# A decoder block on one core: write strength from one narrow product, experts in alternation, smaller VectorE steps, new order tables

## The chip, the cores and the metric

The kernel runs on one core of a Trainium2 chip. A core has TensorE (PE, matrix products into PSUM), VectorE (DVE), ScalarE (ACT), GpSimd (POOL) and SyncE (SP, which issues DMAs here); they run side by side and wait for each other through semaphores. The metric is the device time of one execution in microseconds. Three executions of the kernel before took 1631.0 to 1631.2 us, median 1631.13.

## The reference, cut to what matters

The input x has 4 batches of 1024 tokens with 256 channels. Three sublayers follow one another, each added to x after a layer norm: a gated delta rule with 16 heads of 16 channels, a differential cross attention over 64 context tokens, and a convolution with a mixture of 8 experts and a feed-forward part. The change touches the gates of the first and the sum of the third:

```python
p = hidden @ cond_in_W                      # then a rotating scan over time, and an rms norm: cond
deltas = cond @ delta_W                     # 3 x 256 columns for q, k, v and 16 for beta
bd = bd * jax.nn.sigmoid(beta_ramp_logit)
ctrl = hidden @ ctrl_W + ctrl_b             # q, k, v, decay (16), beta (16), gate (256)
beta = jax.nn.sigmoid(bet_l + bd)           # write strength, one per head and token
g = jax.nn.sigmoid(dec_l)                   # decay, one per head and token
def step(Sst, inp):
    qt, kt, vt, bt, gt = inp
    Sd = gt[..., None, None] * Sst
    kS = jnp.einsum('bhk,bhkv->bhv', kt, Sd)
    Snew = Sd + jnp.einsum('bhk,bhv->bhkv', kt, bt[..., None] * (vt - kS))
    ot = jnp.einsum('bhk,bhkv->bhv', qt, Snew)
    return (Snew, ot)
...
rw = jnp.sum(jax.nn.one_hot(top_i, E, dtype=x1.dtype) * top_w[..., None], axis=-2)
ye = jax.nn.silu(jnp.einsum('bsd,eod->bseo', x1, expert_w) + expert_b)
combined = jnp.einsum('bse,bseo->bso', rw, ye)
```

## The kernel before

The 1024 tokens are cut into 8 blocks of 128 tokens of all 4 batches, 512 columns in the layout with channels on partitions. `turns` walks i from -1 to 8. In turn i three pieces of work are interleaved: the front part of block i+1 (marked + in the table `ORDER`: layer norm, the rotating scan, the projections, the causal convolution), the recurrent part of block i (no mark), and attention and experts of block i-1 (marked -). In turns 1 to 6 all three run. I call turn i "block i"; it ends with `x1_`, VectorE's sum of the residual with the output product of block i (line 1201).

What sets the order of the work is written out by hand: `ORDER` has one list of steps for each engine, and an engine runs its steps in exactly this order, waiting at each for the events that it needs (`up`) and telling its own (`fin`). The table `KEEP` has the program issue dummy products (`keep`, line 1440, a 128x128 product of the identity with itself) ahead of certain steps of TensorE.

The front part has PSUM bank 7 for itself. Each of its products waits until the one before has been read out, so on TensorE they stand far apart and other work lies between. They are `turn1` (transposes), `rot`, `unrot`, `gate`, `cond`, `db` and `proj.0` to `proj.7`. `proj.0` and `proj.1` give the logits of the write strength, each of the 16 columns repeated 16 times, so that `beta` comes out in the layout of k and v (256 rows for 16 heads). `proj.2` to `proj.7` are q, k and v. ScalarE takes exp of the two, VectorE (`beta_`, line 1024) adds one over 128x1024, and ScalarE takes ln and exp of that (`blog`, lines 611 and 612): sigmoid(x) is exp(-ln(1 + exp(-x))). `db` computes the decay logits with tokens on partitions: for each batch two products of `hT` with `ctrl`, one of the condition with `dw`, and one that adds the bias, each of 32 columns. VectorE bounds them (`edb`, line 1051), ScalarE takes exp, and in the next turn, as their first steps, VectorE adds one (`spread`, line 1069), ScalarE takes ln into `lgc` (line 645), and GpSimd expands this into `xpand` and `lrep`, which TensorE's `decay` and `grow` read.

In the recurrent part, `sum.0` to `sum.3` are the products for the norms of q and k (they read squares that ScalarE makes, line 631), `raw.0` to `raw.7` are products of keys with keys and queries, `am` scales them, and `solve.0` to `solve.15` invert a triangular matrix by small VectorE steps. After `solve.15` each of 8 chunks of 16 tokens goes through `z`, `zc`, `d1`, `m`, `cs`, `s`, `co`, `o`: `z`, `d1`, `cs` and `co` are TensorE's, the others VectorE's, and `s` of a chunk gives the state that `d1` of the next reads.

In the third part, `sc`, `max`, `pt`, `pv` and `av` are attention (scores, softmax, transposes, values, VectorE's difference of two attentions), and `moe.0` to `moe.31` the expert products, two for each pair u of experts, u from 0 to 15. ScalarE takes silu of a pair's result into one of four buffers, and VectorE's `acc` adds the pair's two experts to `comb`, the sum of their batch, one instruction each:

```python
b, ep = u // 4, u % 4
up("moe_act", u + 1)
for e2 in range(2):
    ins = stt(comb[:, b, :], src, wgt, comb[:, b, :], ALU.mult, ALU.add)
```

All instructions of four pairs in a row add to the same `comb[:, b, :]`, and each waits for the one before. `o_` and `av` are also chains of four dependent VectorE instructions, each run as one step.

## Time and profile before

| | us |
|---|---|
| median of three executions | 1631.13 |
| the profiled execution | 1631.66 |
| its span, first to last instruction | 1629.9 |
| TensorE busy | 1526.6 |
| VectorE busy | 1220.2 |
| ScalarE busy | 845.6 |
| GpSimd busy | 204.8 |

The span is the time from the first to the last instruction on the core; the execution's own time is 1.8 us longer. Busy time is the time in which an engine ran an instruction. A product of 32-bit numbers appears as two records, so a count of 52 dummy records is 26 products at most; two records of one product overlap, and a distance between starts tells what a product costs in a full stream. Some records of the bias products, in 16-bit numbers, are missing.

### The profile page before, as it was taken

What the parts mean: (1) busy time and instruction counts of PE and PEld (TensorE: products, weight loads), DVE (VectorE), ACT (ScalarE), POOL (GpSimd) and SP (SyncE); (2) the same over time, 40 slices, a digit from 0 to 9 for tenths busy, and PEclk for the clock granted to TensorE, in tenths of its full rate; (3) what the DMA queues carried; (4) which work ended last, traced back from release to release, by engine and by line L of the source; (5) the groups of instructions that cost most, each with busy time, mean ns of one, the idle gap of its engine ahead of it and who ended that gap; (6) DMA issues with size and microseconds to landing.
All of it is one profiled execution on the core that took longest, in us unless ns stands there. A gap on an engine that the chain in (4) does not pass through costs nothing.

```text
span 1629.9 us, 39565 instructions
## 1 busy us (share of the span) xinstructions
PE 1526.6 (94%) x16532; PEld 1040.2 (64%) x16598; DVE 1220.2 (75%) x3201; ACT 845.6 (52%) x1612; POOL 204.8 (13%) x212
## 2 busy tenths in 40 slices
PE   5899899999999999999999999999999999999888
PEld 3475677656766577656765577656766577757665
DVE  6256868886788878886798877877798867875553
ACT  1354454655646474655646474655646474534333
POOL 0030212011300112011300112011200112010000
PEclk7999989999999999999999999999999999999999
DMA  5010001000100001000100001000100001000000
GB/s 228 1 27 27 3 1 28 27 2 14 28 6 23 2 14 27 28 2 15 27 13 16 2 15 27 27 2 4 38 1 15 2 14 28 15 2 14 1 1 13
DMA packets 20217, 31.75 MB, mean 19 GB/s; under 512 B 1480, under 2 KB 17864, under 8 KB 19784
## 3 DMA queue, kind: packets, MB, share of 16 engines
q1 hardware_dynamic: 20040, 29.22, 6.2%
q8 instruction: 132, 2.16, 0.6%
q14 instruction: 45, 0.37, 0.1%
HBM read 20.81 MB, written 8.39 MB: 18 GB/s over the span
## 4 chain that ended last, share of the span: by engine, by line
PE 77%; DVE 17%; ACT 3%; issue 3%; DVEq 0%
PE bank L1781 15%; PE bank L1518 7%; PE bank L1729 6%; PE bank L1397 6%; PE four L1590 4%; PE bank L1440 4%; PE bank L1719 4%; PE bank L1520 3%; PE bank L1422 3%; PE bank L1705 3%; PE four L1642 2%; PE four L1609 2%; PE four L1658 2%; PE bank L1429 2%; PE four L1422 2%
## 5 line engine op out<-in xcount | busy, mean ns | idle before, releaser
L1781 PE MATMUL bank<-w_sb,cs 128*128 128x512 f32 x512 | 257.8, 614 | 0.1
L791 ACT ACTIVATE cs<-bank 128x512 f32<-128x512 f32 x128 | 76.2, 595 | 203.5 <-remote 130.3
L510 POOL TENSOR_TENSOR decayed<-state,pk 128x512 f32<-128x512 f32 x64 | 69.7, 1090 | 716.4 <-DVE state L1165 716.4
L1440 PE MATMUL bank<-c_sb 128*128 128x128 f32 x1070 | 141.1, 286 | 5.3 <-DMA c_sb<-in_consts 5.3
L1440 PEld LDWEIGHTS bank<-c_sb 128*128 128x128 f32 x1070 | 134.4, 200 | 17.7 <-issue 10.9
L1729 PE MATMUL bank<-vx_sb,cs 128*128 128x136 f32 x1024 | 136.7, 286 | 8.1 <-ACT cs L745 8.1
L745 ACT COPY cs<-bank 128x512 f32<-128x512 f32 x128 | 74.9, 585 | 127.0 <-PE bank L1719 127.0
L1345 DVE SCALAR_TENSOR_TENSOR cs<-cs,rwt 128x256 f32<-128x256 f32 x224 | 117.9, 526 | 26.9 <-ACT cs L791 14.8
L1729 PEld LDWEIGHTS bank<-vx_sb,cs 128*128 128x128 f32 x1024 | 125.7, 192 | 17.0 <-ACT cs L745 11.6
L1781 PEld LDWEIGHTS bank<-w_sb,cs 128*128 128x128 f32 x512 | 89.5, 189 | 73.0 <-issue 64.1
L1518 PE MATMUL bank<-hT,w_sb 128*128 128x512 f32 x256 | 124.4, 608 | 9.1 <-ACT pre L595 6.2
L1719 PE MATMUL bank<-c_sb,cs 128*128 128x128 f32 x512 | 81.2, 281 | 22.4 <-ACT cs L745 14.7
L738 ACT ACTIVATE cs<-cs 128x1024 f32<-128x1024 f32 x64 | 67.4, 1052 | 63.8 <-DVE cs L1243 63.8
L1238 DVE TENSOR_REDUCE pkc<-bank 128x8 f32<-128x512 f32 x128 | 82.7, 682 | 21.1 <-PE bank L1705 20.9
L1037 DVE SCALAR_TENSOR_TENSOR qkv<-pre,l_sb,qkv 128x512 f32<-128x512 f32 x144 | 97.5, 746 | 0.0
L1243 DVE TENSOR_TENSOR cs<-bank,pkc 128x512 f32<-128x512 f32 x128 | 81.9, 681 | 20.7 <-PE bank L1719 20.7
L1165 DVE SCALAR_TENSOR_TENSOR state<-four,c_sb,decayed 128x128 f32<-128x128 f32 x256 | 71.9, 344 | 31.7 <-PE four L1642 29.4
L1719 PEld LDWEIGHTS bank<-c_sb,cs 128*128 128x128 f32 x512 | 55.6, 141 | 59.6 <-issue 48.7
L545 ACT ACT_TABLE_LOAD x66 | 84.7, 1283 | 1.2
L1705 PE MATMUL bank<-kbx,cs 32*128 32x256 f32 x512 | 83.6, 400 | 0.2 <-ACT cs L733 0.2
L1397 PE MATMUL bank<-cs,w_sb 128*128 128x256 f32 (+1 forms) x320 | 80.1, 389 | 0.4 <-DVE cs L1290 0.4
L1148 DVE SCALAR_TENSOR_TENSOR shared<-four,c_sb 128x256 f32<-128x256 f32 x128 | 55.5, 475 | 32.8 <-PE four L1609 32.5
(243 smaller groups left out, 2990.5 us busy)
## 6 DMA issues: line engine op xcount, KB each, us to landing
xt<-in_x SPq DMA_DIRECT2D x8, 512.0 KB, 4.8
vscr<-qkv SPq DMA_DIRECT2D x8, 512.0 KB, 2.6
vT<-vscr SPq DMA_DIRECT2D x32, 128.0 KB, 4.4
Tm<-in_x SPq DMA_DIRECT2D x8, 512.0 KB, 3.8
out<-cs SPq DMA_DIRECT2D x8, 512.0 KB, 2.9
w_sb<-in_weights SPq DMA_DIRECT2D x1, 3656.0 KB, 19.1
w_sb<-in_weights SPq DMA_DIRECT2D x1, 1840.0 KB, 9.1
cs<-in_scratch SPq DMA_DIRECT2D x3, 256.0 KB, 9.5
```

Source lines behind the costliest of these rows:

```text
L545: nc.scalar.preload_act_table_set(name)
L1037: ins = stt(dst, pre[:, n % 4, :, t:TB + t], L("conv", 4 * n + t, 4 * n + t + 1), dst, ALU.mult, ALU.add)
L1238: step.append(link(red(mx[:, a, :], sc[a], AX.X, ALU.max)))
L1243: fin("psub", tt(prob[:, 4 * a:4 * a + 4, :, :].rearrange("p h f n -> p f h n"), sc[a].rearrange("p (f h) n -> p f h n", f=2), mx[:, a, :] ...
L1345: ins = stt(comb[:, b, :], src, wgt, comb[:, b, :], ALU.mult, ALU.add)
L1397: last = mm(dst, lhs(k), rhs(k), start=k == 0, stop=k == n - 1)
L1440: mm(bank[7 if i > 0 else 6][:, 0:P], ident, ident, start=True, stop=True)
L1518: last = mm(dst, ctrl[:, k, cc:cc + P], hT[:, k, :], start=k == 0, stop=False)
L1705: last = mm(bank[4 + a][:, 256 * f:256 * f + 256], qx[r:r + 32, f, b * TB:b * TB + TB], kbx[r:r + 32, f, b, :], start=True, stop=True)
L1719: last = nc.tensor.transpose(bank[6][:, h * P:h * P + P], prob[:, 4 * n + h, :, :].rearrange("p f n -> p (f n)"), ident)
L1729: last = mm(bank[6][:, 34 * h:34 * h + 136], probT[:, h, :], vx_sb[:, at:at + 136], start=True, stop=True)
L1781: mm(dst, x1T[:, k, b * TB:b * TB + TB], ew[:, k, ep * 512:ep * 512 + 512], start=k == 0, stop=False)
```

## The change

**Write strength.** `proj` has six steps instead of eight, for q, k and v alone. `db` now computes decay and write strength together as one product with channels on partitions: 32 rows (16 decay, 16 beta) by 512 columns. ScalarE takes exp with the bias in it, VectorE bounds and adds one, ScalarE takes ln; the result `lgT` lies in 32 rows of `rota`. Two new kinds of TensorE steps read it: `btr` transposes it to tokens on partitions for the decay (VectorE copies that into `lgc`), and `brep.0` and `brep.1` multiply it by a constant selector matrix that repeats each of the 16 rows 16 times, after which one exp on ScalarE gives `beta`. All this is in the front part; the steps `spread` of VectorE and ScalarE at the start of the turn, and `beta_`, are gone.

```diff
                 def db():
                     up("cond")
-                    if i == 0:
-                        pe.wait_ge(ld_b3, 48)
-                    for b in range(B):
-                        dst = bank[7][:, b * 32:b * 32 + 32]
-                        for k in range(KC):
-                            mm(dst, hT[:, k, b * TB:b * TB + TB], ctrl[:, k, 1280:1312], start=k == 0, stop=False)
-                        mm(dst, rotb[:, b * TB:b * TB + TB], dw[:, 1024:1056], start=False, stop=False)
-                        last = bias(dst, "db")
-                    fin("db_ps", last)
+                    emptied()
+                    fin("db_ps", controls(bank[7][0:32, :], 1024, 32))
...
+                def btr():
+                    up("lg")
+                    emptied()
+                    for b in range(B):
+                        last = nc.tensor.transpose(bank[7][:, 32 * b:32 * b + 32], lgT[:, b * TB:b * TB + TB], ident[0:32, 0:32])
+                    fin("lt_ps", last)
...
+                def brep(g):
+
+                    up("lg")
+                    emptied()
+                    fin("brep_ps", mm(bank[7][:, :], C("sel")[0:32, P * g:P * g + P], lgT, start=True, stop=True))
```

`controls` is the three products that `proj` also uses. `emptied` waits for whatever step last used bank 7; before, each step named that step itself, so their order was fixed in the code.

**Experts.** A pair u is now of batch 2 * (u // 8) + u % 2, so that neighbouring pairs add to different batches, and a step `acc.u.e2` is one instruction.

```diff
+        def expert(u):
+
+            return 2 * (u // 8) + u % 2, u % 8 // 2
...
+                        if e2:
+                            ch.wait(added[u % 2])
                         else:
-                            if not e2:
-                                up("moe_acc", u)
-                            ins = stt(comb[:, b, :], src, wgt, comb[:, b, :], ALU.mult, ALU.add)
+                            up("moe_acc", u - 1)
+                        ins = stt(comb[:, b, :], src, wgt, comb[:, b, :], ALU.mult, ALU.add)
```

**Smaller steps.** `o_` and `av` are likewise cut into four steps of one instruction each, which the order places singly.

**Order.** `ORDER` and `KEEP` are new throughout; a full turn has 20 dummy products instead of 25, turns -1, 0, 7 and 8 have 103, 140, 51 and 114 instead of 84, 117, 74 and 110. Two lines of TensorE's list:

```diff
-        sum.0 sum.1 decay sum.2 +turn1.0 -turn2.0 +turn1.1 grow -turn2.1 -qx.0 sum.3 -sc.0.0 -qx.1 -sc.0.1 vturn raw.0
...
+        sum.0 sum.1 decay -turn2.0 sum.2 grow -turn2.1 -qx.0 sum.3 -sc.0.0 -qx.1 -sc.0.1 vturn raw.0 raw.1 -sc.1.0
```

TensorE at the seam between two full turns, before. The first row is the output product, 1440 the dummies, 1543 `sum`, 1560 and 1561 `decay`, 1469 `turn1`, 1429 `turn2`, 1568 `grow`:

```order
L1422 MATMUL four<-w_sb,kn 128x256 x8
L1440 MATMUL bank<-c_sb 128x128 x8
L1543 MATMUL four<-rota,c_sb 128x512
L1543 MATMUL four<-rotb,c_sb 128x512
L1560 MATMUL four<-Tm,c_sb 128x512
L1561 MATMUL four<-Tm,c_sb 128x512
L1543 MATMUL four<-rota,c_sb 128x512
L1469 MATMUL bank<-c_sb,xt 128x128 x4
L1429 MATMUL bank<-c_sb,cs 128x128 x4
L1469 MATMUL bank<-c_sb,xt 128x128 x4
L1568 MATMUL four<-c_sb,mk 128x128 x8
```

And now (1441 the output product, 1568 `sum`, 1585 and 1586 `decay`, 1448 `turn2`, 1459 the dummies, 1593 `grow`):

```order
L1441 MATMUL four<-w_sb,kn 128x256 x8
L1568 MATMUL four<-rota,c_sb 128x512
L1568 MATMUL four<-rotb,c_sb 128x512
L1585 MATMUL four<-Tm,c_sb 128x512
L1586 MATMUL four<-Tm,c_sb 128x512
L1448 MATMUL bank<-c_sb,cs 128x128 x4
L1568 MATMUL four<-rota,c_sb 128x512
L1459 MATMUL bank<-c_sb 128x128 x3
L1593 MATMUL four<-c_sb,mk 128x128 x8
```

The dummies ahead of `sum.0` are gone, three stand ahead of `grow`, and `turn1` has moved to a later place.

TensorE around the first step `z.0` of the recurrence in a full turn, before (1518 and 1520 `proj.1`, 1719 `pt.15`, 1415 and 1422 attention's output product, 1609 `z`, 1729 `pv.7`):

```order
L1518 MATMUL bank<-hT,w_sb 128x512 x2
L1520 MATMUL bank<-rotb,w_sb 128x512
L1719 MATMUL bank<-c_sb,cs 128x128 x4
L1415 MATMUL bank<-bias,ones 128x512
L1422 MATMUL bank<-w_sb,cs 128x256 x4
L1609 MATMUL four<-kn,M 32x128 x16
L1729 MATMUL bank<-vx_sb,cs 128x136 x8
```

And now (1514 `cond`, 1746 `pt.11`, 1634 `z.0` and `z.1`, 1756 `pv.5`, 1732 `sc.7`, 1667 `cs.0.0`, 1530 and 1531 the new `db`):

```order
L1514 MATMUL bank<-qkv,c_sb 128x512
L1746 MATMUL bank<-c_sb,cs 128x128 x4
L1634 MATMUL four<-kn,M 32x128 x16
L1756 MATMUL bank<-vx_sb,cs 128x136 x8
L1732 MATMUL bank<-kbx,cs 128x256 x4
L1634 MATMUL four<-spare,M 32x128 x16
L1667 MATMUL four<-rq,shared 64x4x16 x8
L1530 MATMUL bank<-hT,w_sb 32x512 x2
L1531 MATMUL bank<-rotb,w_sb 32x512
```

`z.0` has moved ahead of `db`, all `proj` and the last three steps `pv`.

VectorE in the last scaling step `am.3` and after it, before (1102 to 1104 `am`, 1251 to 1256 `av.2`, 994 and 1000 the scan of the front part, 1116 and 1120 `solve.0`, 1238 and 1243 `max`):

```order
L1104 TENSOR_TENSOR mk<-four,pk 128x2x8x16
L1251 RECIPROCAL pkc<-bank 128x16
L1253 TENSOR_SCALAR pkc<-pkc,small 128x8
L1254 TENSOR_TENSOR cs<-bank,pkc 128x256
L1256 TENSOR_TENSOR cs<-cs 128x128
L994 TENSOR_TENSOR rotb<-bank,sinT 128x512
L1000 SCALAR_TENSOR_TENSOR qkv<-rota,zc,rotb 128x128 x4
L1116 STREAM_TRANSPOSE Tm<-M 128x16x32 x2
L1120 MEMSET Tm 128x4x16
L1238 TENSOR_REDUCE pkc<-bank 128x8 x2
```

And now (987 `turn1`, 1118 and 1122 `solve.0`, 1261 to 1271 the four steps of `av.1`, 1135 and 1139 steps of the solve):

```order
L1106 TENSOR_TENSOR mk<-four,pk 128x2x8x16
L987 COPY hT<-bank 128x512
L1118 STREAM_TRANSPOSE Tm<-M 128x16x32 x2
L1122 MEMSET Tm 128x4x16
L1261 RECIPROCAL pkc<-bank 128x16
L1135 TENSOR_TENSOR M<-Tm 128x56
L1267 TENSOR_SCALAR pkc<-pkc,small 128x8
L1139 TENSOR_TENSOR Tm<-Tm,M 128x4x14
L1269 TENSOR_TENSOR cs<-bank,pkc 128x256
L1135 TENSOR_TENSOR M<-Tm 128x104
L1271 TENSOR_TENSOR cs<-cs 128x128
```

The solve starts two attention steps earlier and its steps alternate with those of `av`.

## Rows read from the trace of the kernel before

**Rows 1.** The page: busy time of the engines, and the chain by engine.

```profile
PE 1526.6 (94%) x16532; PEld 1040.2 (64%) x16598; DVE 1220.2 (75%) x3201; ACT 845.6 (52%) x1612; POOL 204.8 (13%) x212
...
PE 77%; DVE 17%; ACT 3%; issue 3%; DVEq 0%
```

**Rows 2.** Stretch, us, busy PE, PEld, DVE, ACT, POOL (instructions), PE clock, DMA share, GB/s.

```profile
405.90:590.60 184.70, 178.84 (x1982) 119.53 (x1991) 148.63 (x390) 104.24 (x200) 25.53 (x26) 0.99 0.06 16
590.60:773.50 182.90, 177.04 (x1981) 117.71 (x1989) 148.64 (x389) 104.23 (x200) 25.54 (x26) 1.00 0.06 16
```

**Rows 3.** The same of line 1440 alone (dummies), block 3: PE and PEld.

```profile
590.60:773.50 182.90, 6.27 (x52) 5.91 (x51) 1.00 0.06 16
```

**Rows 4.** TensorE's timeline in block 3: start, us, instruction, idle before.

```profile
658.66 0.53 PE L1530 MATMUL bank<-w_sb,hT 128*128 128x32 f32 x4
...
661.37 2.10 PE L1729 MATMUL bank<-vx_sb,cs 128*128 128x136 f32 x16
663.31 1.88 PE L1518 MATMUL bank<-hT,w_sb 128*128 128x512 f32 x4
...
665.88 0.60 PE L1429 MATMUL bank<-c_sb,cs 128*128 128x128 f32 x4
```

**Rows 5.** Timelines at the seam to block 3: TensorE, VectorE, ScalarE, GpSimd.

```profile
590.37 1.95 PE L1440 MATMUL bank<-c_sb 128*128 128x128 f32 x16
592.82 1.12 PE L1543 MATMUL four<-rota,c_sb 128*128 128x512 f32 x2 [0.51 <-ACT rota L631]
...
594.64 1.02 PE L1560 MATMUL four<-Tm,c_sb 128*128 128x512 f32 x2
...
590.57 1.29 DVE L1201 TENSOR_TENSOR xr<-four,Tm 128x512 f32<-128x512 f32 x2 [2.69 <-PE four L1422]
...
591.99 0.26 ACT L645 ACTIVATE lgc<-edb 128x64 f32<-128x64 f32 x1 [5.00 <-DVE edb L1069]
...
592.32 1.22 POOL L470 TENSOR_TENSOR Tm<-lgc,c_sb 128x256 f32<-128x256 f32 x2 [13.04 <-ACT lgc L645]
```

**Rows 6.** The solve's end, `pt.11` and `z.0` in block 3; the page's softmax row.

```profile
667.74 1.93 DVE L1124 STREAM_TRANSPOSE M<-Tm 128x512 f32<-128x512 f32 x2
...
651.88 0.63 PE L1719 MATMUL bank<-c_sb,cs 128*128 128x128 f32 x4 [0.20 <-ACT cs L745]
...
671.98 0.69 PE L1609 MATMUL four<-kn,M 64*32 64x128 f32 x32
...
L1238 DVE TENSOR_REDUCE pkc<-bank 128x8 f32<-128x512 f32 x128 | 82.7, 682 | 21.1 <-PE bank L1705 20.9
```

**Rows 7.** Busy time in three stretches of block 3, columns as in rows 2.

```profile
607.00:635.00 28.00, 28.00 (x380) 22.15 (x381) 19.73 (x44) 15.29 (x35) 10.86 (x13) 1.00 0.19 40
635.00:665.00 30.00, 27.12 (x208) 19.93 (x205) 28.39 (x68) 14.36 (x24) 0.00 (x0) 1.00 0.00 1
...
680.00:695.00 15.00, 15.00 (x205) 9.39 (x204) 13.27 (x36) 10.18 (x18) 1.06 (x1) 1.00 0.01 2
```

**Rows 8.** VectorE's timeline: dependent sums (1345, 1175) and independent ones (1165).

```profile
721.50 3.81 DVE L1345 SCALAR_TENSOR_TENSOR cs<-cs,rwt 128x256 f32<-128x256 f32 x7
...
726.39 1.12 DVE L1175 SCALAR_TENSOR_TENSOR M<-four,c_sb,M 128x128 f32<-128x128 f32 x3
727.59 1.13 DVE L1165 SCALAR_TENSOR_TENSOR state<-four,c_sb,decayed 128x128 f32<-128x128 f32 x4
```

**Rows 9.** TensorE's timeline in block -1: `db`, `proj.0`, `proj.1`.

```profile
46.00 0.63 PE L1530 MATMUL bank<-w_sb,hT 128*128 128x32 f32 x4
...
49.35 1.92 PE L1518 MATMUL bank<-hT,w_sb 128*128 128x512 f32 x4
...
52.91 1.99 PE L1518 MATMUL bank<-hT,w_sb 128*128 128x512 f32 x4 [0.78 <-ACT hid L589]
```

**Rows 10.** ScalarE's timeline around a switch of table.

```profile
691.28 1.28 ACT L545 ACT_TABLE_LOAD   x1
692.58 0.84 ACT L775 ACTIVATE cs<-bank,l_sb 128x256 f32<-128x256 f32 x2
```

362 lines of the change are left out of this document (185 added, 177 removed), and 3 rows, old and new, of the table KEEP.

## The prediction

> **What bounds the kernel now.** The page first: TensorE is busy for 94% of the span, VectorE for 75%, ScalarE for 52%, and in the chain that ended last TensorE has 77% and VectorE 17% [rows 1]. A busy TensorE need not be doing useful work here, because the program also issues dummy products. So I next cut the span at the residual sum `x1_`, which ends a block of 128 tokens. Blocks 1 to 6, where all pipeline halves run, last 182.9 to 184.7 us (three have the clock of the first of rows 2 and 184.4 to 184.7 us, three that of the second and 182.9 to 183.0). Block 3 holds 177.0 us of TensorE in 182.9 us, so 5.9 us are idle [rows 2], and 6.3 us of its busy time are dummies [rows 3]. These 12.2 us I call the slack of a block. VectorE is idle for 34 us of it, so on average TensorE is the bound. It is not so everywhere: from 607 to 635 us TensorE never stops and VectorE has 19.7 of 28 us; from 635 to 665 us VectorE has 28.4 of 30 us and TensorE idles for 2.9 [rows 7].
>
> **The work that goes.** Durations below are distances between starts in a full stream, not busy times. A `proj` (three products of 512 columns) runs from 663.31 to 665.88: 2.57 us, so 2.6. The old `db`, with its 16 small products, runs from 658.66 to 661.37: 2.71 us [rows 4]. Removed per block: two `proj` and the old `db`, 2 x 2.6 + 2.7 = 7.9 us. Added: a `db` of the same three 512-column products with only 32 output rows. The trace shows no product of this form; above stands `proj` with 2.6, below the old `db` less its four bias products, about 2; I take 2.6, since the columns that stream are the same. Two selector products contract over 32 rows; the nearest rows are `sum.0` and `sum.1` (512 columns each), which start at 592.82 and are done when `decay` starts at 594.64, so 1.8 for two [rows 5]. Four transposes of 32 columns are not in the trace either: above, four of 128 columns take 0.60 us [rows 4], below, nothing; I take 0.5, as each loads weights like those. Sum 4.9, **saved 3.0 us per block** (2.9 to 4.1 with the ends). It counts where TensorE is the bound, in blocks 1 to 6: 18 us.
>
> ScalarE loses two passes over 128x1024 and gains a few over 32x512, VectorE trades one pass over 128x1024 and two over 128x64 for one over 32x512 and one copy. Both engines have idle time for that; I cost it at nothing, and count what it does at the seam below. Where ScalarE's cover is gone, as in block -1, it is worth under 1 us.
>
> **The seam between blocks.** After the output product ends (about 590.4) TensorE runs eight dummies and then idles 0.51 us before `sum.0` at 592.82. What ended this wait is ScalarE's square at 592.15, and ahead of that in ScalarE's queue stands the logarithm of the decay at 591.99, which waits for VectorE's `edb`, behind `x1_` [rows 5]. The change takes this logarithm to the block before, so the square no longer waits for `x1_`, and `sum.0` and `sum.1` can follow the output product at once. Next late is `decay`: it needs GpSimd's expansion, which now starts after `x1_` itself (591.86) rather than at 592.32 and takes 1.2 us, so about 593.1 to 593.2 instead of 594.64. TensorE waits there for 1 us or so. The seam gives back 1.4 us; `turn1`, which filled part of it, goes to a later place, so in slack I credit 0.6 us.
>
> **VectorE's stretch.** `z.0` needs the end of the triangular solve (two transposes, 667.74 to 669.67) and started at 671.98 [rows 6]. In the new order the solve starts before the fourth softmax step and its steps lie between those of the attention sums, so that VectorE's waits from 607 to 635 us (8.3 us by rows 7) fill with it. Two softmax steps (four passes of the kind of line 1238 each, 82.7 / 128 = 0.65 us a pass, 2.6 us), two attention sums (four dependent small instructions, 1.2 to 1.6 us by rows 8) and two small steps, some 8 us together, come behind the solve. The solve then ends 16 us or so earlier in the block, near 653, and TensorE gets to the new place of `z.0` at about the same time (its old neighbour `pt.11` stood at 651.88). Splitting helps too: three dependent sums of 128x128 take 1.12 us, four independent ones 1.13, so 0.39 against 0.26 us from start to start, while expert sums stand at 3.81 / 7 = 0.54 us each [rows 8]. If the same 0.13 us goes from each, alternation between two batches saves up to 32 x 0.13 = 4 us of VectorE per block, the interleaving of the attention sums with the solve perhaps 2. VectorE is idle elsewhere, so this reaches the time only through the 2.9 us that TensorE idles from 635 to 665 us and the short waits before expert products. I take 1.2 us.
>
> **Dummies.** 20 instead of 25 per block, each 0.24 us of TensorE (52 records, 6.27 us, two records each): 1.2 us, if the waits that they covered are gone.
>
> Slack thus falls by 0.6 + 1.2 + 1.2 = 3.0 of 12.2 us (bounds -1 and 8), and a full block by 6.0: **6 x 6.0 = 36 us**.
>
> **The ends.** In block -1 everything goes through bank 7 in turn, product and read-out. The old `db` holds it from 46.00 to 49.35, each of the two write-strength products 3.56 us (49.35 to 52.91, 0.78 of it the read-out) [rows 9]: 10.5 us. New: `db` 2.6 + 0.8, the transposes with VectorE's copy 0.9, two selector products with read-out 2 x 1.7: 7.7. Gain 2.8, less 0.3 for the logarithm over 32x512 where one over 128x64 stood: 2.5 us. Block 0 is set by the recurrence; half of the 3.0 us, less half of what 23 more dummies cost, is nothing (range 4 either way). Block 7 has no next block, so no work is removed; 23 dummies less are worth between 0 and 5.5 us, I take 2. Block 8: nothing, 2 either way.
>
> Sum: 36 + 2.5 + 2 = 40.5. The profiled execution took 1631.66 us, 1.8 above its span and 0.5 above the median of 1631.13. 1631.66 - 40.5 = 1591.2, or 1590.6 on the median's footing: **1591 us**.
>
> **A rule that speaks against it.** The new ScalarE order switches to the table of silu, back for the logarithm and to silu again shortly before `pw.0`, two more switches there and two fewer at the tail. A switch takes 1.28 us and the next operation starts 1.30 us after it (691.28 to 692.58) [rows 10]. ScalarE has 4.8 of 15 us free there, from 680 to 695 us [rows 7], so 2.6 us are hidden. The Trainium skill's page "ScalarE: Activation LUTs" (section "What ACT_TABLE_LOAD costs") states 1283 ns plus a drain of about 1380 ns, 2.66 us for each switch. The first part agrees with the row, the drain is not to be seen in it. By the row the sum stands at 1591; by the page, the two switches would be 5.3 us, and if the 2.7 us more lay on the path of all six blocks, 1607.
>
> **Rivals.**
> (a) *More slack goes.* If the solve fills VectorE's waits fully and the expert sums stop holding ScalarE, slack falls by 6 instead of 3: 6 x 3 = 18 us more, 1573. For it: TensorE's needs are met by VectorE alone from 635 to 665 us. Against: some of the 5.9 us idle are short gaps after missing records of the bias products, which no order removes.
> (b) *Only the work goes.* Slack stays at 12.2 us, because `z.0` and its recurrence now stand in the stretch where VectorE had 28.4 of 30 us, and what the seam gains is waited for at `decay` and `grow`. Gain 18 + 2.5 = 20.5, thus 1611.
> (c) *The queue turns against it; slower.* `z.0` now stands ahead of `pv.5` and of the scores behind it in TensorE's queue. If VectorE's 8.3 us of waits are not filled, the solve ends 8 us after TensorE arrives. Each block then loses 8.3 us at that place against 3.0 saved and 1.2 of dummies: 6 x 4.1 = 25 us more, 1656. It decides from a wait of 4.2 us at `z.0` on. Against it: `raw.7`, on which the solve's input rests, also stands some six steps earlier.
> (d) *Nothing happens*: a loop through VectorE sets each block and the saved products become waits or dummies; 1631. Against: from 607 to 635 and from 680 to 695 us TensorE is busy without a gap [rows 7].
> (e) *The clock*: fewer useful products and no dummies where the order guesses wrong let TensorE's granted clock fall to its lower level once in each block, as in three of the six now, which are 1.5 us or more longer [rows 2]. Three more blocks cost 4.5 us: inside the range of the forecast, so no case of its own.
>
> **How the numbers follow.** Forecast 0.52; (a) 0.20; (b) 0.19; (c) 0.05; (d) 0.04. The forecast's own terms move by 6 x 0.5 for the work, 6 x 2 for slack about it and 4 for the ends, so 1580 to 1605; the range takes in most of (b) and half of (a): **1576 to 1611**. A measurement of this kernel can tell 0.2%, about 3 us, from no change. Faster: the forecast, (a), (b): 0.91. Same: (d): 0.04. Slower: (c): 0.05.
>
> **What would show it.** In the changed profile: full blocks of 176 to 179 us between `x1_` and `x1_`; `sum.0` right behind the output product and 1 us or so of idle before `decay`; the transposes that end the solve some 60 to 62 us after `x1_` instead of 77, and less than 1 us of idle before `z.0`; dummies 20 per block; expert sums near 0.4 us each. I am wrong if TensorE's idle time per block exceeds 8 us (then look before `z.0`, `decay`, `grow` and in the tail behind the last expert product, where three chunks of the recurrence now stand instead of two), or if `db` takes much more or less than 2.6 us.

## The result and the profile after

The changed kernel takes **1622.11 us** (median of 5 runs, 1616.38 to 1627.61) against 1631.13 (5 runs beside it, 1630.29 to 1634.54): ratio 0.9941, interval 0.9913 to 0.9968. It is faster by 9 us, not by the 40 that were forecast, and outside the range. A second set of 6 runs, made beside the later experiments, gave 1617.57 us (0.9921, interval 0.9900 to 0.9942). The profiled execution is the slowest of the first set, 1627.61 us, with a span of 1625.8.

The page of the changed kernel, the lines that answer to [rows 1]:

```profile
PE 1519.0 (93%) x16376; PEld 1024.8 (63%) x16376; DVE 1179.9 (73%) x3193; ACT 830.7 (51%) x1594; POOL 209.2 (13%) x212
...
PE 72%; DVE 22%; ACT 3%; issue 3%; POOL 0%; DVEq 0%; ACTq 0%
```

VectorE did less (1180 for 1220 us), yet its share of the chain grew from 17% to 22%. The blocks 1 to 7 of the changed kernel, from `x1_` to `x1_`, columns as in [rows 2]:

```profile
219.15:403.74 184.59, 176.93 (x1953) 116.19 (x1952) 143.35 (x388) 102.63 (x198) 26.37 (x26) 0.98 0.06 16
403.74:588.52 184.78, 177.15 (x1953) 116.23 (x1952) 143.40 (x388) 102.55 (x198) 26.34 (x26) 0.98 0.06 16
588.52:769.85 181.33, 173.71 (x1953) 114.53 (x1952) 143.19 (x388) 102.56 (x198) 26.36 (x26) 1.00 0.06 16
769.85:953.02 183.17, 175.58 (x1953) 115.36 (x1952) 143.26 (x388) 102.66 (x198) 26.36 (x26) 0.99 0.06 16
953.02:1137.63 184.61, 176.95 (x1953) 116.22 (x1952) 143.34 (x389) 102.66 (x198) 26.36 (x26) 0.98 0.06 16
1137.63:1322.37 184.74, 177.06 (x1953) 116.13 (x1952) 143.34 (x388) 102.54 (x198) 26.37 (x26) 0.98 0.05 13
1322.37:1488.34 165.97, 155.38 (x1938) 111.74 (x1937) 121.41 (x331) 81.35 (x163) 23.03 (x25) 0.98 0.06 14
```

Two things are to be seen. Only block 3 had TensorE's full clock, and it lasts 181.3 us, where the like block before lasted 182.9 (second of [rows 2]): **1.6 us less, not 6.0**. And the others are longer by 1.7 us for each fall of the granted clock to 1.2 GHz. One fall lasts 3.4 us here, so it takes 0.01 from the mean clock of a block: two falls at 0.98, one at 0.99, nine in blocks 1 to 6, where before there were three. In the profiled run those six extra falls ate all that the six blocks had gained: they last 1103.2 us together, before 1102.4.

What is left of the gain stands outside the six blocks. The stretch up to `x1_` of block 0, in the kernel before, the changed kernel and its second profile (`after_again`, below), columns as in [rows 2]:

```profile
0.00:222.96 222.96, 182.19 (x1974) 125.43 (x1975) 133.71 (x357) 85.34 (x154) 25.84 (x29) 0.92 0.15 52
0.00:219.15 219.15, 185.31 (x2005) 127.92 (x2006) 131.60 (x357) 83.73 (x153) 25.46 (x29) 0.93 0.15 52
0.00:212.41 212.41, 177.79 (x2005) 123.39 (x2006) 131.45 (x357) 83.58 (x153) 25.43 (x29) 0.97 0.15 53
```

TensorE was at the lower clock for 34.1, 30.7 and 13.7 us of it. If each such microsecond costs half a microsecond, the most it can, the three stretches would last 206, 204 and 206 us at the full clock (an estimate from these rows). So the 4 to 11 us gained there are mostly clock, and a gain of the change itself is not shown there.

The new steps on TensorE in block 3, `db`, `btr` and `brep.0` (start, us, instruction):

```profile
657.36 1.90 PE L1530 MATMUL bank<-hT,w_sb 128*32 128x512 f32 x4
...
668.30 0.43 PE L1550 MATMUL bank<-c_sb,rota 32*128 32x32 f32 x4
...
669.64 1.12 PE L1558 MATMUL bank<-rota,c_sb 32*128 32x512 f32 x2
```

`db` runs until `pt.12` at 660.06: 2.7 us. The next steps start 0.36 us behind `btr` and 1.05 behind each `brep`. Added: 2.7 + 0.4 + 2.1 = 5.2 for a forecast of 4.9; saved 7.9 - 5.2 = **2.7 us of work, against 3.0**. This term held.

The seam at 588.52, the answer to [rows 5]:

```profile
588.32 1.02 PE L1568 MATMUL four<-rota,c_sb 128*128 128x512 f32 x2
...
591.24 1.13 PE L1585 MATMUL four<-Tm,c_sb 128*128 128x512 f32 x2 [1.03 <-POOL Tm L481]
...
596.34 2.02 PE L1593 MATMUL four<-c_sb,mk 128*128 128x128 f32 x16 [1.16 <-DVE pk L1084]
```

`sum.0` stands right behind the output product, `decay` waits 1.03 us for GpSimd, as forecast, and starts 2.7 us behind `x1_` (4.1 before). But `grow` waits another 1.16 us for VectorE.

From `x1_` to `pt.4`, to `pt.11` and to the block's end, first the kernel before, then the changed one (both block 3, full clock):

```profile
590.57:626.97 36.40, 35.42 (x388) 27.02 (x386) 29.18 (x72) 24.73 (x55) 10.59 (x13) 1.00 0.15 30
626.97:651.88 24.91, 23.23 (x188) 15.44 (x185) 22.53 (x53) 9.90 (x16) 2.47 (x3) 1.00 0.00 1
651.88:773.53 121.65, 118.44 (x1409) 75.31 (x1419) 96.96 (x266) 69.59 (x129) 12.47 (x10) 1.00 0.05 15
```

```profile
588.52:627.72 39.20, 36.72 (x414) 27.77 (x413) 34.88 (x83) 23.48 (x52) 13.12 (x16) 1.00 0.13 28
627.72:651.77 24.05, 20.87 (x148) 13.72 (x149) 23.53 (x62) 13.09 (x24) 0.00 (x0) 1.00 0.00 1
651.77:769.85 118.08, 116.12 (x1392) 73.05 (x1392) 84.78 (x245) 65.99 (x122) 13.24 (x10) 1.00 0.05 15
```

TensorE idles 2.5 us up to `pt.4` (1.0 before), 3.2 to `pt.11` (1.7 before) and 2.0 behind it (3.2 before; 1.3 us of that are nine gaps of 0.15 us where records are missing, see `before_less_work`). With 4.95 us of dummies (line 1459, 40 records) for 6.27 [rows 3], the slack of a block is 12.6 us, where it was 12.2. It was to fall by 3.0.

### The profile page after: what moved, and what is told of

The parts are those of the page before. It is cut to its first block, busy times and chain, and to the rows that moved or that the text cites. A ratio compares the mean times of both kernels' runs of the same rounds, so it can differ in the third digit from the quotient of the medians.

```text
span 1625.8 us, 39269 instructions
## 1 busy us (share of the span) xinstructions
PE 1519.0 (93%) x16376; PEld 1024.8 (63%) x16376; DVE 1179.9 (73%) x3193; ACT 830.7 (51%) x1594; POOL 209.2 (13%) x212
## 4 chain that ended last, share of the span: by engine, by line
PE 72%; DVE 22%; ACT 3%; issue 3%; POOL 0%; DVEq 0%; ACTq 0%
PE bank L1808 14%; PE bank L1756 6%; PE bank L1530 5%; PE bank L1416 5%; PE bank L1746 4%; PE bank L1459 4%; PE bank L1732 4%; PE four L1615 4%; PE bank L1441 3%; PE bank L1531 2%; PE four L1634 2%; PE bank L1523 2%; PE four L1683 2%; DVE qkv L1038 2%; PE bank L1422 2%
## 5 line engine op out<-in xcount | busy, mean ns | idle before, releaser
L1808 PE MATMUL bank<-w_sb,cs 128*128 128x512 f32 x512 | 246.9, 602 | 0.0
L521 POOL TENSOR_TENSOR decayed<-state,pk 128x512 f32<-128x512 f32 x64 | 74.4, 1163 | 925.5 <-DVE state L1167 925.5
L1808 PEld LDWEIGHTS bank<-w_sb,cs 128*128 128x128 f32 x512 | 95.1, 191 | 90.9 <-issue 80.1
L1364 DVE SCALAR_TENSOR_TENSOR cs<-cs,rwt 128x256 f32<-128x256 f32 x224 | 98.7, 482 | 70.2 <-ACT cs L797 70.1
L1530 PE MATMUL bank<-hT,w_sb 128*128 128x512 f32 (+1 forms) x224 | 109.7, 613 | 6.2 <-ACT pre L598 4.0
L1732 PE MATMUL bank<-kbx,cs 32*128 32x256 f32 x512 | 87.4, 400 | 0.7 <-ACT cs L739 0.7
```

Of the source, the lines that this page charges most:

```text
L1530: mm(dst, ctrl[:, k, at:at + n], hT[:, k, :], start=k == 0, stop=False)
L1732: last = mm(bank[4 + a][:, 256 * f:256 * f + 256], qx[r:r + 32, f, b * TB:b * TB + TB], kbx[r:r + 32, f, b, :], start=True, stop=True)
L1808: mm(dst, x1T[:, k, b * TB:b * TB + TB], ew[:, k, ep * 512:ep * 512 + 512], start=k == 0, stop=False)
```

## The experiments

Sixteen more runs were made, one of them of the changed kernel again. Each kernel is compared with the kernel before on the same chip; the medians of that one were 1631.1 to 1633.6 us.

**1. The clock.** The theory to test: falls of the granted clock, brought on by many short waits of TensorE, ate the gain. `after_again` is the changed kernel as it is.

> The changed kernel unchanged, beside the others on this chip. If the falls of the clock come by where a block happens to stand when the chip looks, then this profile shows the same three places (47, 119 and 170 us behind x1_) in other blocks than the first profile did, and the runs spread over 6 us or more again, in the order of their mean granted clock, 1.4 to 1.5 us for each 0.001 of it. If they are this kernel's own, each in its block, the falls stand in the same blocks as before.

1617.57 us (1615.54 to 1623.44). The falls stood 47, 119 and 170 us behind `x1_` again, but in blocks 2, 4 and 5, five of them, where the first profile had them in 1, 2, 4, 5 and 6. The eleven runs of both sets follow their mean clock closely, though not in strict order, from 0.979 with 1627.61 to 0.987 with 1615.54 to 1616.38: some 1.4 us per 0.001, and one fall is 0.001. So the place of a fall belongs to the kernel, and whether it happens is another matter in each block and run.

`after_dummies_in_waits`:

```diff
+KEEP = {(1, -1, "pt", 5): 1, (1, -1, "pv", 2): 2, (1, -1, "pt", 6): 2, (1, -1, "pt", 7): 3,
+        (1, -1, "pt", 9): 2, (1, 0, "d1", 6): 2, (1, 0, "co", 7, 0): 1,
...
```

> The changed kernel with 13 dummies more in each of blocks 1 to 6, put where TensorE waits anyway: ahead of pt.5 (1), pv.2 (2), pt.6 (2), pt.7 (3), pt.9 (2), d1.6 (2) and co.7.0 (1). In the changed kernel's profile the granted clock falls to 1.2 GHz nine times in these blocks, seven of them 47 and 170 us behind x1_. The clock theory says that these falls ate the gain: the seven go, each is worth 1.7 us (a block with none lasts 181.3, with one 183.1, with two 184.7), so 12 us less than the profiled run of the changed kernel and 6 to 8 less than its median: 1614 to 1616. The rival, new waits ate it: falls or not, blocks do not get shorter than 181.3 us, and the median moves by under 3 us, because in the median run of the changed kernel the clock is about that of the kernel before.

1609.86 us (1607.28 to 1613.29), ratio 0.9874 (0.9855 to 0.9893). Five blocks last 181.4 to 181.5 us, one 183.1 with one fall. In the changed kernel's block 1, the 6.8 us ahead of the fall and the fall itself; then the same place with the dummies (columns as in [rows 2]):

```profile
259.60:266.40 6.80, 4.74 (x35) 3.78 (x36) 6.52 (x17) 2.23 (x3) 0.00 (x0) 1.00 0.00 0
266.40:269.80 3.40, 3.40 (x8) 1.63 (x6) 2.43 (x5) 1.82 (x3) 0.00 (x0) 0.51 0.02 5
```

```profile
252.20:259.00 6.80, 6.48 (x51) 5.57 (x51) 6.52 (x17) 2.23 (x4) 0.00 (x0) 1.00 0.01 2
259.00:262.50 3.50, 3.50 (x22) 2.54 (x21) 3.46 (x8) 1.89 (x3) 0.00 (x0) 1.00 0.00 0
```

TensorE was busy for 4.74 of 6.8 us, in pieces between waits, and its clock fell; with 6.48 us it did not. The median is 8 to 12 us under the changed kernel's two. The profiled runs differ from its two by 8.3 and 20.3 us; the six blocks hold 5.9 and 13.0 us of that, and the stretch up to block 0, where these dummies do not stand, 0.6 and 7.4. Blocks got no shorter than 181.4, so the clock explains nothing of the 26 us by which six full blocks miss the forecast (6 x 6.0 less 6 x 1.6).

`after_no_dummies` drops the three entries of `KEEP` for blocks 1 to 6.

> The changed kernel without its 20 dummies in blocks 1 to 6 (4.5 us of TensorE per block). If they only stand in waits, a block with a full clock stays at 181.3 us and idle time takes their place (7.8 to 12.3 us idle per block), and what changes is the clock: falls at the seam behind x1_ come on top, one or two in each block, 6 x 1.7 to 12 x 1.7 us, so 1632 to 1642. The rival, dummies cost what they last: 6 x 4.5 = 27 us less, 1595.

1628.79 us (1625.87 to 1637.86, 12 runs). Idle time took the place of the dummies (11.7 us per block for 7.6 and 5.0), and there were 13 falls in the six blocks, four of them of 6.8 us. In block 1, where the first fall stands 176 us behind `x1_`, the last expert product starts 154.6 us behind `x1_` in both kernels and the output product 177.5 us (177.7 with the dummies): the dummies cost at most 0.2 us of a block, and they buy 7 to 11 us of clock. My third slack term, "5 fewer dummies 1.2 us", was thus worth nothing: what a dummy covers is a wait.

**2. The new VectorE steps.** `after_steps_together`, in VectorE's order:

```diff
-... solve.0 -av.1.0 solve.1.0 -av.1.1 solve.1.1 ... o.1.0 -av.7.0 o.1.1 -av.7.1 o.1.2 ... -acc.0.0 -acc.1.0 -acc.0.1 -acc.1.1
+... solve.0 -av.1.0 -av.1.1 -av.1.2 -av.1.3 solve.1.0 ... o.1.0 o.1.1 o.1.2 o.1.3 -av.7.0 ... -acc.0.0 -acc.0.1 -acc.1.0 -acc.1.1
```

> The changed kernel with the four steps of each attention sum, the four of each chunk's output and the two of each expert sum put together again on VectorE, at the place of the first. It undoes the interleaving alone. If finer steps are worth what I gave them (0.13 us for each dependent step, 32 expert sums and the attention sums: 4 to 6 us of VectorE per block, 1.2 us of the time), a full block lasts 182.5 us and VectorE is busy 5 us more of it: about 7 us more than the changed kernel, 1629. If VectorE's slack takes it, under 2 us.

1638.53 us (12 runs), ratio 1.0026 (1.0006 to 1.0047): 0.3% slower than the kernel before. Its stretches from `pt.4` to `pt.11` and the whole block 3:

```profile
620.70:647.04 26.34, 21.05 (x149) 13.88 (x149) 25.33 (x64) 13.10 (x24) 0.00 (x0) 1.00 0.00 1
...
581.55:765.98 184.43, 174.00 (x1950) 114.69 (x1952) 147.61 (x389) 102.79 (x198) 25.57 (x26) 1.00 0.06 16
```

A block at full clock lasts 184.4 us: interleaving is worth **3.1 us**, of which 2.3 between `pt.4` and `pt.11`, where VectorE works 1.8 us longer and TensorE waits 2.1 us more. I had given it 1.2 in all. (The order was made for single steps; what an order made for whole steps would take was not tried, so 3.1 us is what interleaving is worth in this order.)

`after_no_alternation`:

```diff
-            return 2 * (u // 8) + u % 2, u % 8 // 2
+            return u // 4, u % 4
...
-                            up("moe_acc", u - 1)
+                            up("moe_acc", u)
```

> The changed kernel with experts in the old order, all of one batch before the next, and each expert's two sums one behind the other, as they then must be. If the alternation is what keeps ScalarE's read-out of the experts, and so TensorE, from waiting, TensorE idles again behind router.0, 0.5 us or more in each block, and the median is 3 to 6 us over the changed kernel's. My sum held VectorE idle enough there: nothing, within 2 us at the same clock.

1623.34 us at clocks of 0.982 to 0.988. Blocks 1, 3 and 5 last 183.9 us with one fall, where the changed kernel's blocks with one fall last 182.9 to 183.2: 0.7 to 1.0 us per block for the alternation. On VectorE the expert sums of the changed kernel stand closer:

```profile
720.50 2.45 DVE L1364 SCALAR_TENSOR_TENSOR cs<-cs,rwt 128x256 f32<-128x256 f32 x6
722.87 0.34 DVE L1181 SCALAR_TENSOR_TENSOR M<-four,c_sb,M 128x128 f32<-128x128 f32 x1
```

That is 2.45 / 6 = 0.41 us each, where seven dependent ones took 0.54 [rows 8]. Over the whole run the median distance from start to start of neighbouring sums is 0.40 us, 0.52 before and 0.52 again in `after_no_alternation`. So the 0.13 us for each sum came as forecast. (One sum still lasts 0.48 us; neighbours that do not wait for each other overlap.) It takes 2 us off VectorE in a block, and 0.7 to 1.0 us of that reach the time.

**3. Where TensorE's work counts.** `before_less_work` leaves out two of the three products of each write-strength projection of the kernel before:

```diff
+                    if j < 2:
+                        fin("proj_ps", mm(dst, ctrl[:, 0, cc:cc + P], hT[:, 0, :], start=True, stop=True))
+                        emptied[0] = ("pre_sb", i, j + 1)
+                        return
```

> The kernel before, in its own order, with each of its two 128-wide write-strength products cut from five passes of matmul to one of 512 columns: about 2 x 2.1 = 4.3 us of TensorE per block less, nothing added or moved; the write strength it computes is not that of the reference. If TensorE's work reaches the time one for one, as my sum had it: 6 x 4.3 = 26 us and some 4 more in block -1, 1601 to 1605. If VectorE's and ScalarE's chains around them set the pace, most of it turns into waits: 1620 or more.

1616.89 us (1610.97 to 1624.23), ratio 0.9910 (0.9886 to 0.9934). Its block 3, full clock:

```profile
582.72:763.52 180.80, 175.21 (x1982) 116.23 (x1981) 148.52 (x389) 104.28 (x200) 25.54 (x26) 1.00 0.06 16
```

180.8 for 183.0 us. My expectation had the cut too large: a projection has three products, and between starts it now takes 0.85 and 0.93 us (655.51 to 656.36, 657.63 to 658.56) for 2.57 and 2.67, so 3.4 us are gone and not 4.3. **2.2 of the 3.4 us arrive**; most of the rest stands as two new waits behind the cut, 0.20 us ahead of a softmax transpose and 0.84 ahead of `z.0`. This kernel also shows the dense expert products and their neighbours with almost no gap, where the trace of before has nine gaps of 0.15 us each, 1.3 us, with nothing changed there: records are missing. So the true slack before was about 11 us rather than 12.2, and it rose by more than the 0.4 us above.

`after_less_late`, `after_less_tensor`, `after_less_vector` and `after_less_both` cut work in the changed kernel:

```diff
-                    for k in range(KC):
+                    for k in range(1 if at < 768 else KC):
                         mm(dst, ctrl[:, k, at:at + n], hT[:, k, :], start=k == 0, stop=False)
```

```diff
-                    fin("rot_ps", over_k(bank[7][:, :], lambda k: cin[:, k, n * P:n * P + P], lambda k: hT[:, k, :]))
+                    fin("rot_ps", mm(bank[7][:, :], cin[:, n, n * P:n * P + P], hT[:, n, :], start=True, stop=True))
...
-                        step.append(link(red(mx[:, a, :], sc[a], AX.X, ALU.max)))
+                        step.append(link(red(mx[:, a, :], sc[a][:, :, 0:NK // 4], AX.X, ALU.max)))
```

(the gate likewise with one product; the first cut is `after_less_late`, the second `after_less_tensor`, the third `after_less_vector`.)

> The changed kernel with the six projections of one product less each (the second half of the contraction left out, so q, k and v are not the reference's): 6 x 0.86 = 5.2 us of TensorE less in each block, between 662 and 701 us of block 3, where TensorE has 39.2 of 40 us and VectorE 33.5. That is where the removed products stood. If TensorE is the bound there, blocks of 176.1 us. If the work behind it waits for VectorE again, a part goes into waits: half, as in the kernel before with two shorter products (2.2 of 4.3 us), would be 178.7 us.

1609.36 us, 0.9856 (0.9831 to 0.9881). From `pt.11` to `turn3.1` and on to `moe.8`, the changed kernel, then this one. By the order, four of the shortened projections (`proj.0` to `proj.3`) lie in the first stretch and two in the second:

```profile
651.77:689.98 38.21, 38.01 (x597) 24.16 (x596) 29.86 (x81) 23.35 (x47) 3.18 (x3) 1.00 0.10 30
689.98:716.01 26.03, 25.43 (x266) 15.63 (x261) 22.19 (x71) 15.02 (x25) 1.16 (x1) 1.00 0.01 1
```

```profile
635.69:671.25 35.56, 34.79 (x588) 22.59 (x587) 29.71 (x81) 22.84 (x47) 3.18 (x3) 1.00 0.11 32
671.25:699.02 27.77, 25.52 (x257) 15.38 (x257) 22.25 (x71) 15.02 (x25) 1.16 (x1) 0.94 0.00 1
```

In the first, 2.6 of 4 x 0.86 = 3.4 us arrive; TensorE idles 0.8 us for 0.2, since `z.5` now waits 0.58 us for VectorE. In the second, of 1.7 us nothing does: without its fall of 1.7 us it would last 26.1 us, as before the cut, with 2.3 us idle for 0.6. The longest of its new waits is `d1.4`'s, for VectorE's state:

```profile
682.22 0.46 PE L1651 MATMUL four<-state,kq 64*32 64x64 f32 x32 [1.14 <-DVE state L1167]
```

So of the 5.2 us cut from a block 2.6 arrive, in one part of it.

> The changed kernel with rot.0, rot.1, gate.0 and gate.1 of one product instead of two, so the gate and the rotated input are not the reference's; nothing is moved. 4 x 0.9 = 3.6 us of TensorE's work less in each block, all of it between 624 and 649 us of block 3, in the same stretch as in after_less_vector. If VectorE sets that stretch, the 3.6 us turn into idle time of TensorE and the blocks stay at 180.5 to 181.3 us. If TensorE's work reaches the time as my sum had it, blocks of 177.7 us, 22 us less than the changed kernel, about 1600.

> The changed kernel with both maximum passes of each softmax step over a quarter of the scores (16 of 64 keys per head), so the maxima are not the true ones; nothing is moved. Each of the 16 passes of a block goes from 0.65 to some 0.25 us: 0.4 us x 14 = 5.6 us less VectorE between x1_ and pt.11, where it is busy 17.1 of 19.5, 24.8 of 27 and 27.8 of 30 us. If VectorE sets that stretch, TensorE's 3.2 us of waits between pt.4 and pt.11 go and a full block falls from 181.3 to 178 to 179 us: 14 to 20 us less than the changed kernel, 1602 to 1608. If TensorE's own work or ScalarE sets it, blocks stay within 0.5 us of 181.3.

> The changed kernel with both cuts at once: the maximum passes over a quarter of the scores, and rot.0, rot.1, gate.0, gate.1 of one product each. Alone they gave full blocks of 180.9 and 181.2 us. If two bounds of nearly the same length stand side by side from raw.7 to pt.11 (TensorE's work with its waits for ScalarE's copies, and the loop through VectorE), both together give 2 to 4 us: blocks of 177.5 to 179.5 us. If a third thing sets it, the round trip of the transposes, the copies and the product in PSUM bank 6, it stays at 180.5 to 181 us.

`after_less_tensor` gave 1619.55 us (12 runs) and `after_less_vector` 1613.97 (7 runs), but their clocks differ (0.965 to 0.984 and 0.976 to 0.991), so the blocks at full clock are compared: 181.2 and 180.9 us, against 181.3. Neither 3.6 us less on TensorE nor some 5.5 us less on VectorE is worth more than 0.4 us.

A fall tells the same from the other side. Block 1 of `after_less_tensor` has one, 47 us behind `x1_`, in the stretch that lost the work:

```profile
211.99:393.44 181.45, 172.12 (x1942) 114.20 (x1944) 143.16 (x388) 102.62 (x198) 26.33 (x26) 0.99 0.06 16
```

It costs 0.2 us, where the fall at that place costs 1.4 to 1.7 us in the changed kernel (blocks with it and the one 170 us behind `x1_` last 184.6, with the latter alone 182.9 to 183.2). So in the changed kernel more work on TensorE costs its full time there and less work gives nothing: TensorE is one of two bounds of nearly the same length.

`after_less_vector`, from `pt.4` to `pt.11` and the whole block 3:

```profile
618.03:642.00 23.97, 20.81 (x148) 13.79 (x149) 21.52 (x62) 13.07 (x24) 0.00 (x0) 1.00 0.00 1
...
579.06:759.93 180.87, 172.94 (x1950) 113.94 (x1952) 137.73 (x388) 102.51 (x198) 26.34 (x26) 1.00 0.06 16
```

Both cuts together gave 1607.39 to 1636.94 us, at mean clocks from 0.981 down to 0.960. In the profiled run (0.961) four blocks have 13.7 us in a row at 1.2 GHz, and only block 6 had the full clock.

```profile
1146.50:1326.80 180.30, 170.08 (x1945) 112.40 (x1944) 137.75 (x388) 102.66 (x198) 26.34 (x26) 1.00 0.05 13
```

180.3: 1.0 us for 9 us of work, when I had expected 2 to 4 or nothing. VectorE's 23.5 of 24 us had looked like the bound of the stretch from `pt.4` to `pt.11`, and it is not the only one. What stands there can be read from TensorE's timeline of the changed kernel:

```profile
627.72 0.63 PE L1746 MATMUL bank<-c_sb,cs 128*128 128x128 f32 x4
...
629.12 0.63 PE L1746 MATMUL bank<-c_sb,cs 128*128 128x128 f32 x4 [0.38 <-ACT cs L751]
630.42 2.12 PE L1756 MATMUL bank<-vx_sb,cs 128*128 128x136 f32 x16 [0.68 <-ACT cs L751]
...
634.11 0.63 PE L1746 MATMUL bank<-c_sb,cs 128*128 128x128 f32 x4 [0.50 <-DVE cs L1271]
635.50 0.63 PE L1746 MATMUL bank<-c_sb,cs 128*128 128x128 f32 x4 [0.77 <-ACT cs L751]
```

One PSUM bank goes round: transposes, ScalarE's copy, transposes, copy, the attention product, VectorE's sum, and again the transposes of the next step. From `pt.4` to `pt.6` that is 6.4 us: the steps of one loop in a row, which no engine's busy share shows. The next two rounds, from `pt.6` and `pt.8`, take 8.4 and 7.8 us, since TensorE has `rot.1`, the gates and `unrot` in them and VectorE the scan. In block 6 of `after_less_both` the three rounds take 6.3, 8.0 and 7.2 us, and the first step of each new round waits for VectorE's sum, with both cuts in:

```profile
1191.76 0.63 PE L1745 MATMUL bank<-c_sb,cs 128*128 128x128 f32 x4 [0.42 <-DVE cs L1271]
...
1199.74 0.63 PE L1745 MATMUL bank<-c_sb,cs 128*128 128x128 f32 x4 [1.03 <-DVE cs L1271]
```

So the round without other work does not get shorter by either cut, and the other two shorten by 0.5 and 0.6 us.

**4. Orders that should have filled the waits.** `after_filled_order` and `after_split_products`, in TensorE's order:

```diff
-... -pt.6 -pt.7 +rot.1 -pv.3 ... +gate.0 -pt.8 -pt.9 +unrot -pv.4
+... -pt.6 +rot.1 -pt.7 -pv.3 ... +gate.0 -pt.8 +unrot -pt.9 -pv.4
```

> The changed kernel with two TensorE steps moved by one place: rot.1 between pt.6 and pt.7 (it stood behind pt.7), unrot between pt.8 and pt.9 (it stood behind pt.9). In block 3 of the changed kernel pt.7 waits 0.77 us and pt.9 0.85 us for ScalarE's copy of the transposes just before. If TensorE's own order makes these waits, they go, 1.6 us in each of blocks 1 to 6, of which some comes back: blocks of 180.0 instead of 181.3 us, and with fewer falls of the clock 47 us behind x1_, 1610 to 1614. If VectorE sets that stretch (27.8 of 30 us busy), the waits only move to pv.3 to pt.11 and z.0, the blocks stay at 181.3 us, and only the falls change: 1615 to 1622.

1619.24 us, full block 181.7: slower by 0.4. The waits ahead of `pt.7` and `pt.9` went, and 0.67 us each stand ahead of `pv.3` and `pv.4`, which wait for the second copy. I had moved the filler from one hole to the other.

```diff
-... -pt.6 -pt.7 +rot.1 -pv.3 ... +gate.0 -pt.8 -pt.9 +unrot -pv.4
+... -pt.6 +rot.1.0 -pt.7 +rot.1.1 -pv.3 ... +gate.0.0 -pt.8 +gate.0.1 -pt.9 +unrot -pv.4
```

> The changed kernel with the two products of rot.1 and of gate.0 apart: one ahead of pt.7 (pt.9), one behind it, so that each of ScalarE's two copies of a softmax step has a product of 0.93 us beside it, where in the changed kernel one copy in two has none. Nothing is left out. The waits of 0.77 and 0.85 us ahead of pt.7 and pt.9 go without others in their place if TensorE is one of the bounds there; if the loop through VectorE is right behind, as the cut of TensorE's work suggests, the block gains 0 to 0.4 us, 181.0 to 181.3, and the waits stand ahead of pt.6, pt.8 and pt.10 for VectorE's attention sum instead.

1615.15 us (1612.67 to 1624.35), full block 181.5. Both holes are filled, and the next bound comes up:

```profile
625.37 0.63 PE L1754 MATMUL bank<-c_sb,cs 128*128 128x128 f32 x4
...
632.42 0.63 PE L1754 MATMUL bank<-c_sb,cs 128*128 128x128 f32 x4 [1.51 <-DVE cs L1271]
```

`pt.7` waits for nothing, and `pt.8` waits 1.51 us for VectorE's attention sum. So the loop through VectorE is as long as TensorE's path to within some tenths of a microsecond.

`after_own_expansion_first`:

```diff
-        xpand = Tm[:, 0:2, :, :].rearrange("p a b c -> p (a b c)")
+        xpand = sb("xpand", [P, 512])[:, :]
...
-                        pool.wait_ge(ev["x1"].sem, ev["x1"].at(i - 1))
+                        pool.wait_ge(ev["gsum_ps"].sem, ev["gsum_ps"].at(i - 1))
+                        pool.wait_ge(ev["mkq"].sem, ev["mkq"].at(i - 1, 8))
...
-        -ln2.0.0 -ln2.0.1 -ln2.1.0 dsel -ln2.1.1
+        -ln2.0.0 -ln2.0.1 dsel -ln2.1.0 -ln2.1.1
```

> The changed kernel with a buffer of its own for GpSimd's expansion of the decay, which shared one with the residual and so waited for x1_, and with VectorE's dsel one step earlier, ahead of ln2.1.0. In the changed kernel decay waits 1.03 us for the expansion and grow 1.16 us for VectorE behind it. If that shared buffer is what the seam waits for, decay starts right behind sum.1 and dsel some 0.9 us earlier: 1 to 2 us less in each block, 8 to 14 us less than the changed kernel. If VectorE's own work from x1_ to raw.0 (17.1 of 19.5 us busy) sets the seam, decay's wait goes and grow's grows, and a block stays at 181.3 us.

1622.97 us (1611.93 to 1625.19), full block 181.4. In its timeline `decay` (588.06) follows `sum.1` without a wait, and the wait has split up among the steps behind it:

```profile
590.30 0.66 PE L1449 MATMUL bank<-c_sb,cs 128*128 128x128 f32 x4 [0.36 <-DVE cs L964]
...
593.03 2.02 PE L1594 MATMUL four<-c_sb,mk 128*128 128x128 f32 x16 [0.41 <-DVE pk L1085]
595.22 0.66 PE L1449 MATMUL bank<-c_sb,cs 128*128 128x128 f32 x4 [0.17 <-DVE cs L964]
596.68 1.56 PE L1417 MATMUL bank<-cs,w_sb 128*128 128x256 f32 x6 [0.80 <-ACT cs L729]
```

The expansion was late, but VectorE's layer norm and decay steps behind `x1_` are the bound of the seam.

**5. Faster kernels.** `after_gelu_first`, in TensorE's order and in ScalarE's:

```diff
-... co.7.1 -ffu.0 -ffd.1 onorm.0 onorm.1
+... co.7.1 -ffd.1 -ffu.0 onorm.0 onorm.1
-... -turn6.1 osq.1 -ffd.1 onorm.0 onorm.1
+... -turn6.1 -ffd.1 osq.1 onorm.0 onorm.1
```

> The changed kernel with ffd.1 ahead of ffu.0 on TensorE and the gelu of ffd.1 ahead of the square of osq.1 on ScalarE. At the end of block 3 ScalarE runs the square at 758.90, the gelu at 759.44, a table load at 759.91 and the first rms factor at 761.20; TensorE fills the wait for it with 34 records of dummies. If the end of a block is set by this chain through ScalarE, the gelu's 0.45 us leaves it: 0.4 to 0.5 us per block, 7 to 8 blocks, 3 to 4 us less than the changed kernel. If TensorE's own queue sets it (dummies of 1.8 us ahead of ffu.1), nothing moves.

1610.68 us (1609.99 to 1621.32), 0.9886 (0.9863 to 0.9910). Full blocks last 181.1 us, so the chain gave 0.2 us per block, some 2 us in all. The rest came by the clock: the runs have 0.982 to 0.990 for 0.979 to 0.987, and the profile has no fall from 34 us up to block 3. The same clock of 0.982 gave 1621.32 here and 1623.44 in `after_again`. Against my expectation the mechanism gives half, and what looks like 11 us is mostly another pattern of falls.

`after_dummies_gelu_copy` joins the dummies and the gelu, and lets ScalarE copy `turn1.1` out of PSUM for i > 0 (a second `nc.scalar.copy` in its `turn1`, VectorE's left out). `after_best_split` adds the split products and drops the dummies ahead of `pt.7` and `pt.9`.

> A kernel meant to beat both: the changed kernel with the 13 more dummies in waits, with ffd.1 and its gelu first, and with the copy of turn1.1 out of PSUM (0.68 us of VectorE) on ScalarE, which is idle for half of that stretch. The dummies gave 1610 and the gelu alone blocks of 181.1 us; if VectorE sets the stretch up to pt.11, the copy is worth up to 0.6 us more per block: blocks of 180.5 us and a median of 1602 to 1607. If TensorE's order or the clock alone counts, blocks of 181.1 us and 1607 to 1609.

> A kernel meant to beat after_dummies_gelu_copy (1606.8 us): the same with the two products of rot.1 and gate.0 apart as in after_split_products, and without the dummies ahead of pt.7 and pt.9, in whose place they stand. With the copy of turn1.1 off VectorE and the holes filled, blocks of 180.0 to 180.6 us if both bounds move, 1600 to 1605; 181.1 us and 1606 to 1608 if the loop through VectorE holds.

**1606.84 us** (4 runs, 1605.07 to 1609.25), ratio 0.9850 (0.9827 to 0.9874): the fastest kernel of this study, 24 us under the kernel before. Its blocks are 181.1 us, so the copy gave nothing, and the number came out as the clock alone had it. `after_best_split` gave 1613.51 us (1611.51 to 1616.16): the blocks at full clock have 181.2 to 181.9 us, and with fewer dummies the falls came back (three in six blocks, one of them of 6.8 us).

## Why the prediction was wrong

The six full blocks carried 36 of the 40.5 us.

| step of the prediction | forecast | measured |
|---|---|---|
| work removed, per block | 3.0 us | 2.7 us |
| slack, per block | -3.0 us | +0.4 by the same rows, 1 to 2 us by corrected ones |
| a full block | 176 to 179 us | 181.3 at full clock |
| falls of the clock in blocks 1 to 6 | "three more", 4.5 us | six more in one profile, two more in the other: 3 to 9 us |
| up to `x1_` of block 0 | -2.5 us | 222.96 to 219.15, in the second profile 212.41; mostly clock, by the estimate above |
| block 7 | -2 us | 165.26 to 165.97 |
| expert sums, start to start | 0.54 to near 0.4 us | 0.52 to 0.40 us |

- **The step that failed first is "Slack thus falls by 3.0".** Its three parts: the seam gave nothing (idle ahead of `pt.4` rose from 1.0 to 2.5 us, since `grow` now waits too); the five dummies gave nothing: a dummy covers a wait (`after_no_dummies`); and what interleaving gave was larger than I took (3.1 us by `after_steps_together`), but it was spent. Against the kernel before, the new order without it is 1.4 us longer per block (184.4 for 183.0), although 2.7 us of work are gone. I credited the interleaving as a gain on top of an order that I had judged neutral.
- **The step behind it: removed work "counts where TensorE is the bound, in blocks 1 to 6".** I had judged that by the stretches of [rows 7] in which TensorE never stops. By `after_less_late` three quarters of what is taken out between `pt.11` and `turn3.1` count, and nothing of what is taken out behind; by `after_less_tensor` nothing counts ahead of it either; by `before_less_work` 2.2 of 3.4 us arrived at the place where the products really stood. A stretch without idle time shows that TensorE is late there, not that what follows will be ready sooner.
- **The solve** went as forecast, and nothing came of it. Its closing transposes start at 650.41, 61.9 us behind `x1_` (77 before, forecast 60 to 62), and `z.0` at 652.43 waits for nothing, so rival (c) fell. But VectorE is busy 25.8 of 28 us from 607 to 635 us (19.7 before, [rows 7]), and TensorE, which never stopped there, now idles 2.1 us. From 635 to 665 us it idles 1.4 us, all of it ahead of `z.0`, for 2.9 before. The wait has moved forward in the block, and grown.
- **The clock, case (e),** was named and priced about right (1.5 us each), and then put "inside the range, no case of its own". With it as a case beside (b) the sum would have been 1611 + 3 to 9 = 1614 to 1620, near the result. The nearest case was in fact (b), "only the work goes", with a part of the work lost too. The forecast says that its range takes in most of (b), but (b) stood at 1611, the range's upper end: any fall of the clock on top of it lay outside.
- **The table loads** of the rule that spoke against the change did no harm. A full block has eight of them, as before, three of them between 691 and 702 us of block 3, the first of which reads

```profile
691.27 1.28 ACT L556 ACT_TABLE_LOAD   x1
692.57 1.15 ACT L629 ACTIVATE qkv<-qkv 128x512 f32<-128x512 f32 x2
```

Here too the trace does not show the drain that the Trainium skill states ("ScalarE: Activation LUTs", section "What ACT_TABLE_LOAD costs"): the next operation starts 1.30 us after the load's start, and the row decides. From 690 to 716 us TensorE has one wait of more than 0.15 us, 0.38 us, and VectorE ended it.

What stays open: why the same place has its fall in one block and none in the next, and whether anything of the time up to block 0 (212 to 219 us in the profiles of one kernel) is the change's own. Why both cuts together gave only 1.0 us was traced to the loop through one PSUM bank and VectorE by the timelines; a kernel with a second bank for it was not tried, so that the loop is the cause is argued and not shown.
